# First stage of a latent-attention block: rotated key sums and doubled query columns on GpSimd, first absorbed weights two tiles later

## The reference

```
h   = layernorm(x)
q   = rmsnorm(h @ Wq_a, w) @ Wq_b                    # rank 192 -> 32 heads x (128 + 64)
ckv = h @ Wkv_a                                      # 64 latent + 64 rotary columns
kv  = rmsnorm(ckv[:, :64], w) @ Wkv_b                # 32 heads x (128 key + 128 value)
q_pe, k_pe = rope(q[..., 128:]), rope(ckv[:, 64:])
p   = softmax(causal([q_nope, q_pe] @ [k_nope, k_pe].T * 192**-0.5))
x   = x + layernorm((p @ v) @ Wo)
x   = x + layernorm(w2(silu(w1(x)) * w3(x)))         # each linear layer with a low-rank part
```

## Time and profile before

| | |
|---|---|
| median of 3 runs | 637.61 us |
| the profiled execution | 637.57 us |
| its span, first to last instruction | 635.8 us |
| mean granted TensorE clock | 0.991 |
| PE busy | 603.3 us, 95% |
| DVE busy | 522.8 us, 82% |
| ACT busy | 419.0 us, 66% |
| POOL busy | 133.6 us, 21% |
| first stage up to the last turned latents (L1145 of tile 7) | 46.65 us |

### The profile page before, as it was taken

How to read it: one execution, slowest core, us unless ns; L and a number is a source line. 1 busy time by engine, 2 the same in 40 slices (tenths; PEclk the granted TensorE clock), 3 DMA queues, 4 the chain that set the end, 5 groups by cost and what they waited for, 6 DMA issues and landing times.

```text
span 635.8 us, 12431 instructions
## 1 busy us (share of the span) xinstructions
PE 603.3 (95%) x3432; PEld 446.3 (70%) x3432; DVE 522.8 (82%) x1315; ACT 419.0 (66%) x1165; POOL 133.6 (21%) x124
## 2 busy tenths in 40 slices
PE   4778999999999999999999999999999999899996
PEld 4666767777677677776777777767678888675664
DVE  5897788888888888888888888888877888889456
ACT  4456768777778787777777777878873545265343
POOL 2011122213222222222222322223000000025620
PEclk9998999999999999999999999999999999999999
DMA  8000201202112022021120220203283000001003
GB/s 318 26 1 1 84 23 62 82 0 82 38 45 82 3 79 77 6 82 37 45 82 0 82 57 25 82 29 124 84 276 145 1 1 1 29 1 51 1 16 117
DMA packets 13862, 37.80 MB, mean 59 GB/s; under 512 B 1328, under 2 KB 1584, under 8 KB 13584
## 3 DMA queue, kind: packets, MB, share of 16 engines
q1 hardware_dynamic: 13840, 37.53, 17.5%
HBM read 31.24 MB, written 6.29 MB: 59 GB/s over the span
## 4 chain that ended last, share of the span: by engine, by line
PE 77%; DVE 13%; issue 4%; ACT 3%; DMA 2%; SPq 0%; ACTq 0%; DVEq 0%
PE bank L1027 13%; PE bank L986 13%; PE bank L988 13%; PE bank L987 13%; PE bank L1039 13%; PE bank L1057 3%; PE bank L1049 2%; PE bank L996 2%; DVE dot L838 2%; PE bank L1010 2%; PE bank L1009 2%; DVE ss L638 1%; DMA sq<-sq 1%; PE bank L1204 1%; DVE st L812 1%
## 5 line engine op out<-in xcount | busy, mean ns | idle before, releaser
L362 ACT ACTIVATE pr<-ss,small 128x128 f32<-128x128 f32 (+3 forms) x256 | 143.2, 559 | 41.4 <-DVE small L638 40.7
L370 ACT ACTIVATE pt<-bank 128x128 f32<-128x128 f32 (+3 forms) x256 | 110.9, 433 | 61.2 <-PE bank L1027 60.9
L638 DVE CUSTOM_DVE_ANT_0 ss<-bank,cst 128x128 f32<-128x128 f32 (+3 forms) x256 | 123.2, 486 | 13.8 <-PE bank L988 9.5
L1027 PEld LDWEIGHTS bank<-ident,pr 128*128 128x128 f32 x640 | 75.7, 142 | 66.7 <-ACT pr L362 34.0
L1027 PE MATMUL bank<-ident,pr 128*128 128x128 f32 x640 | 119.0, 284 | 3.1 <-ACT pr L362 3.0
L286 POOL TENSOR_TENSOR qrot<-qrot,qswp 64x512 f32<-64x512 f32 x64 | 82.8, 1293 | 138.4 <-DVE qrot L624 138.4
L986 PE MATMUL bank<-kt_hi,qt_hi 128*128 128x128 f32 (+3 forms) x256 | 101.0, 394 | 3.6 <-DVE qt_lo L628 2.7
L1039 PE MATMUL bank<-pt,kvn 128*64 128x256 f32 (+3 forms) x512 | 86.2, 448 | 0.7 <-ACT pt L370 0.7
L988 PE MATMUL bank<-kt_hi,qt_lo 128*128 128x128 f32 (+3 forms) x256 | 83.3, 325 | 0.0
L987 PE MATMUL bank<-kt_lo,qt_hi 128*128 128x128 f32 (+3 forms) x256 | 83.1, 325 | 0.0
L628 DVE TENSOR_TENSOR qt_lo<-qrot,qt_hi 128x512 fp32r<-128x512 f32 x64 | 60.3, 942 | 24.6 <-ACT qt_hi L352 24.5
(11 more groups left out here) (168 smaller groups left out, 1133.2 us busy)
## 6 DMA issues: line engine op xcount, KB each, us to landing
sv<-sv SPq DMA_DIRECT2D x16, 576.0 KB, 3.7
sq<-sq SPq DMA_DIRECT2D x16, 448.0 KB, 3.4
wvo_scratch<-vs SPq DMA_DIRECT2D x16, 256.0 KB, 2.1
wv_raw<-wvo_scratch SPq DMA_DIRECT2D x8, 512.0 KB, 4.2
xa<-x SPq DMA_DIRECT2D x8, 256.0 KB, 5.9
x<-x SPq DMA_DIRECT2D x1, 2048.0 KB, 10.7
out<-yo SPq DMA_DIRECT2D x8, 256.0 KB, 2.0
w<-w SPq DMA_DIRECT2D x1, 1376.0 KB, 13.1
```

The costliest lines, as they stand in the source:

```text
L362: nc.scalar.activation(pr[:, k % 4, 0:n], ss[:, k % 2, 0:n], ACT.Exp, bias=negmax[:, k % 8:k % 8 + 1], scale=-1.0, accum_out=rsum[:, k:k + ...
L370: nc.scalar.activation(pt[:, b, h, 0:i + 1, i * P:(i + 1) * P], bank[2 + k % 2][:, 0:(i + 1) * P].rearrange("p (j q) -> p j q", q=P), ACT. ...
L638: nc.vector.tensor_tensor_reduce(out=ss[:, k % 2, 0:n], in0=bank[k % 2][:, 0:n], in1=mask[:, SEQ - n:SEQ], scale=-SCALE, scalar=3.4e38, op ...
L1027: last = nc.tensor.transpose(bank[2 + k % 2][:, j * P:(j + 1) * P], pr[:, k % 4, j * P:(j + 1) * P], ident[:, :])
```

## The change

- POOL takes over L765 (the sum of the rotated halves) and, as a copy, L760: columns 128 to 191 of qn, scaled by L759, are copied to 192 to 255. New semaphores `q_scaled` (DVE to POOL) and `q_doubled` (POOL to PE); L762 now raises `qn_made`, and a product waits for `qn_made` before it overwrites its bank.
- `add_rotated` of the first two heads stands behind the sum and copy of tiles 6 and 7, and POOL waits for each to end.
- `absorb_query(0)` moves from before product 0 (step 2) to behind product 2 (step 4) and writes bank 6; `weights_hi(0)` moves to step 4, `weights_lo(0)` to step 5. L1145 of tile 0 no longer waits for `wq_split`.
- SP issues x tiles 4 to 7 before sq.

```diff
+    def absorbed(w):
+        return bank[6 if isinstance(w, int) and w == 0 else XB]
...
-            sp.dma_start(sq[:, :], sq_d[0]).then_inc(a.sq_in, 16)
             for t in range(4, TB):
                 sp.dma_start(xa[:, t, :], xb[t]).then_inc(x_in[t], 16)
+            sp.dma_start(sq[:, :], sq_d[0]).then_inc(a.sq_in, 16)
...
-            for h in range(2):
-                add_rotated(h, h)
+            for t in range(3, TB + 3):
+                if 0 <= t - 3 < TB:
+                    u = t - 3
+                    pool.wait_ge(f.krot_parts, 3 * (u + 1))
+                    nc.gpsimd.tensor_tensor(kvn[:, u, RKV:P], kra[:, u, :], krb[:, u, :], ALU.add).then_inc(f.kvn_made, 1)
+                    pool.wait_ge(f.q_scaled, u + 1)
+                    nc.gpsimd.tensor_copy(qn[:, u, RQ:2 * P], qn[:, u, P:RQ]).then_inc(f.q_doubled, 1)
+                if t in (TB + 1, TB + 2):
+                    pool.wait_ge(f.q_doubled, t - 2)
+                    add_rotated(t - TB - 1, t - TB - 1)
+                    pool.wait_ge(a.pe_added, t - TB)
...
-                if t == 2:
+                if t == 4:
                     weights_hi(0, first=True)
...
-                    nc.vector.scalar_tensor_tensor(qn[:, u, 0:RQ], lat[:, 0:RQ], rq, lnw[:, 0:RQ], ALU.mult, ALU.mult)
-                    nc.vector.scalar_tensor_tensor(qn[:, u, RQ:2 * P], lat[:, P:RQ], rq, lnw[:, P:RQ], ALU.mult, ALU.mult)\
-                      .then_inc(f.qn_made, 1)
+                    nc.vector.scalar_tensor_tensor(qn[:, u, 0:RQ], lat[:, 0:RQ], rq, lnw[:, 0:RQ], ALU.mult, ALU.mult)\
+                      .then_inc(f.q_scaled, 1)
                     nc.vector.scalar_tensor_tensor(kvn[:, u, 0:RKV], lat[:, RQ:RQ + RKV], rc, lnw[:, RQ:RQ + RKV],
-                                                   ALU.mult, ALU.mult)
-                    dve.wait_ge(f.krot_parts, 3 * (u + 1))
-                    nc.vector.tensor_tensor(kvn[:, u, RKV:P], kra[:, u, :], krb[:, u, :], ALU.add).then_inc(f.kvn_made, 1)
+                                                   ALU.mult, ALU.mult).then_inc(f.qn_made, 1)
...
-                if t == 2:
+                if t == 5:
                     weights_lo(0)
...
                     pe.wait_ge(f.kvn_made, u + 1)
-                    if u == 0:
-                        pe.wait_ge(a.wq_split, 1)
+                    pe.wait_ge(f.q_doubled, u + 1)
...
-                if t == 2:
-                    absorb_query(0)
...
                     if u >= 2:
-                        pe.wait_ge(f.kvn_made, u - 1)
+                        pe.wait_ge(f.qn_made, u - 1)
...
+                if t == 4:
+                    absorb_query(0)
```

More of the change, by code:

```diff
@@ L200, in build @@
         x_turned xt_hi_made xt_split wa_hi_made wa_split lat_made squares_summed std_rms_made rstd_rms_made
-        qn_made krot_parts kvn_made qk_turned qk_hi_made qk_split""")
+        q_scaled q_doubled qn_made krot_parts kvn_made qk_turned qk_hi_made qk_split""")
     x_in = [nc.alloc_semaphore(f"x_in{t}") for t in range(TB)]
@@ L340, in weights_hi @@
                     act.wait_ge(a.q_made, 4 * w)
-                pv = bank[XB][:, 0:4 * RKV].rearrange("p (k h n) -> p k h n", k=2, h=2)
+                pv = absorbed(w)[:, 0:4 * RKV].rearrange("p (k h n) -> p k h n", k=2, h=2)
                 rv = sq[:, SQ_COLS - 4 * ROPE:SQ_COLS].rearrange("p (k h n) -> p k h n", k=2, h=2)
@@ L995, in absorb_query @@
                     for h in range(2):
-                        last = nc.tensor.matmul(bank[XB][:, (2 * k + h) * RKV:(2 * k + h + 1) * RKV],
+                        last = nc.tensor.matmul(absorbed(w)[:, (2 * k + h) * RKV:(2 * k + h + 1) * RKV],
                                                 sq[:, (2 * h + k) * P:(2 * h + k + 1) * P],
```

## The result

| | before | changed kernel |
|---|---|---|
| median | 636.57 us (20 runs, 635.61 to 638.52) | 635.57 us (20 runs, 633.85 to 637.71) |
| ratio to before | | 0.998, 95% interval 0.9971 to 0.999 |
| profiled execution, its span | 637.57, 635.8 us | 637.71, 635.9 us |
| last turned latents (PE, tile 7) | 46.65 us | 46.90 us |

The kernel is faster by about 1.3 us (what the ratio takes off 636.6; the medians lie 1.0 apart), 0.2%, which is within the 0.3% that the prediction called no change; it forecast 1.9 us.

The account below looks back on a forecast made before the run. The prediction took TensorE (PE, busy 95% of the span) to bound the kernel, so an earlier attention start carries through. Its terms summed to -1.91, 637.6 - 1.9 = 635.7 us, with an 8 in 10 range of 634.6 to 637.3.

Parts of the forecast that it names:

- pure offset: Before attention: if attention starts x us earlier, everything behind it is x us earlier, since PE is busy 95% of the span.
- the rival that pair 0 gives it back: Pair 0, where VectorE and PE wait in turn: the earlier start is lost there, 637.6 us; chance 0.1.
- Points 1 and 3: Product 0 starts without the absorbed weights, -2.07; VectorE loses L760 and L765, 0.32 per tile, -1.28 -0.20 -0.32.
- point 3: VectorE loses L760 and L765, 0.32 per tile: -1.28 over four tiles, -0.20 for tile 4, -0.32 for tile 6.
- Points 4 and 5: GpSimd's sum and copy per tile: hidden in tiles 0 to 6, -0.16 in tile 7; xn stalled on the port pair, +0.28.
- Point 6: weights_hi(0) on ScalarE moves into the loop between deviation and squares: +0.71 once, bounds 0.71 and 1.3.
- Point 7: weights_lo(0) on VectorE, between L749(2) and L749(3), takes 1.23 with 0.1 to spare: +1.13, bounds 1.0 and 1.23.
- Point 8: add_rotated of heads 0 and 1 on GpSimd, behind tiles 6 and 7's sum and copy: hidden, taken at nothing.
- Point 2: Load of sq behind four x loads in SP's queue: lands near 14, wanted near 20; nothing, with 6 us of cover.
- The rival on the clock: PE's gap opened by weights_lo lowers the granted clock, slowing product 4 and the turning behind it: +0.7, 636.4 us; chance 0.2.

Follow-up runs that it names:

- first variant: The changed kernel with the move undone: GpSimd's sum and copy alone, absorbed weights, their split and the load of sq where they stood before; 634.65 us, ratio 0.9966.
- variant with the second copy: GpSimd's part alone, absorbed weights as before, plus one more GpSimd copy of 64 columns beside xn for tiles 0 to 5; 634.55 us, ratio 0.9967.

## Why the prediction was right, and where it was off

**PE's chain and the pure offset.** From the last turned latents to the end of the span before took 635.8 - 46.65 = 589.1 us. The changed kernel takes 589.0, the variants from 588.6 to 589.6. What the stage gains or loses arrives at the end, to half a microsecond; the rival that pair 0 gives it back is refuted.

**Points 1 and 3.** The start gave 1.99 in the variant with the move alone, whose loads and clock there were those of before (2.07 summed). A tile is 3.67 in place of 4.00: 0.33 (0.32 summed). The first variant bears out the rest of point 3 as well: nothing between tiles 4 and 5 (3.01 and 3.02), then 0.22 (4.85 in place of 5.07, where 0.20 was taken) and 0.33 (4.18 in place of 4.51, where 0.32 was).

**Points 4 and 5.** GpSimd's sum takes 0.32 and its copy 0.24, near what was drawn from the earlier trace rows; the sum was put at 0.4, from a mean of 0.91 in which one sum, begun beside xn, took 1.05 and the others 0.87. The -0.16 for the last tile was -0.04 (1.37 in place of 1.41 in the first variant). The copy ends at 16.30 as xn starts at 16.29, and xn keeps 0.55: the +0.28 for the port pair was 0, since the copy was over before xn could meet it. The stall of 0.65 on the xn at the start lasts until the sum beside it has ended; a copy that ends as xn starts has nothing of that kind to give. The Trainium skill, "SBUF — State Buffer", section "Who interferes with whom", has the engine that comes second fully blocked. The traces agree that xn is blocked beside a sum of 320 columns (its end 0.28 behind the sum's, in ten profiles of ten). Which of the two came first can't be read off the starts shown: in the kernel before, xn starts at 7.29 and the sum that it ended behind at 7.34. The variant with the second copy doesn't test the rule.

**Point 6.** 0.71 for weights_hi, measured 0.71 in the loop (a step of 4.41 against 3.67 and 3.67 again when it is moved into idle time). **Point 7.** 1.13 for weights_lo; the step grew by 4.72 - 3.67 = 1.05. **Point 8.** GpSimd's sum of head 0 ended at 43.81. ScalarE waited for it, as was said, and VectorE did not: qt_lo (44.93) and the last reciprocal (45.53) have no idle time before them. Hidden. The changed kernel:

```profile
43.84 0.63 ACT L365 ACTIVATE qt_hi<-qrot 128x512 fp32r<-128x512 f32 x1 [2.08 <-POOL qrot L290]
```

**Point 2.** Hidden, with 7.3 us of cover where 6 were given.

**What was off.** The rival on the clock was given a chance of 0.2 and a price of 0.7 us. By the mean clocks it holds in about 14 of 20 executions and costs 1.6 us (636.0 against 634.4); that the slower group is gone when the gap is filled supports the reading, and one profile shows it. The sum put this cost at nothing, and that is its one large miss. In the profile the price is 1.06 in the step from tile 3 to 4 (4.73 against 3.67 with the gap filled) and 0.80 in the next (3.80 against 3.00). The prediction had worked out 0.7 for the whole: it let the low clock end with product 4 and the turning behind it, and it lasted into product 5, so the next step grew too. The changed kernel's profiled stage ends at 46.90 instead of the 44.7 predicted: 0.66 of these 2.2 us is the later load of x tile 1, 1.86 is the clock, and 0.3 was gained back in terms priced too high, the port's above all. Where the clock does not fall the sum held: 634.4 is 2.2 us below before, 1.91 summed, and with the port's 0.28 taken out it is 2.19. The predicted 635.7 is near the measured 635.57 by some luck: the kernel gained 1.0 to 1.3 us and not 1.9, and before's median turned out 1 us lower than the one it was built on.

**What each half is worth.** GpSimd's part alone gains more than the whole change: 2.2 us by its ratio against 1.3, with intervals that just overlap. The move of the absorbed weights as it was made costs about 1 us: alone it is 1.2 us slower than before (interval 1.0006 to 1.0033). It gains 2.0 at the start, spends 0.7 + 1.05 in two steps that had no room, and opens the gap in which the clock falls.

## What to carry to other kernels

In a stage that repeats with a fixed step, work taken out of an idle start and put into a step was paid almost in full (weights_hi took 0.71 us and cost 0.73, weights_lo took 1.21 and cost 1.05); ask first which engine has idle time in that step, and at which place of its list (0.7 us came back by moving four activations ahead of the wait, and 1 us more by sharing four subtractions over three steps and two engines). Price a new gap of TensorE by the clock of what follows it as well as by its length, and for executions in which the clock falls and in which it does not: the median mixes the two. Compare the kernels by the lead at one landmark, but first take off what a DMA and the rise of the clock did in that execution: 0.66 and 0.50 us here, where whole effects were 1 to 2 us. When one engine can hold up another, compare the ends of the two instructions over several profiles before pricing the overlap of their starts.

## What the runs showed of the hardware

Work that nobody needs can pay: 2.0 us of matmuls in a gap held the granted clock at 1.00 and removed the slower group of executions. Beside GpSimd's sums of 320 columns a VectorE tensor_scalar of 512 columns ended 0.28 us behind the sum in every one of ten profiles, and so took 0.67 to 1.23 us in place of 0.55; the sum that began beside it took 1.04 to 1.05 in place of 0.87. A GpSimd copy of 64 columns (0.24 us) that began 0.06 us ahead of the same tensor_scalar, and ended before its last 0.28 us, slowed nothing. A gap of 2.2 us on PE was followed by a granted clock of 0.50 in one profile and of 1.00 in another. The same load of 256 KB ended 0.66 us apart in two executions of nearly the same start, half of the effect under study.
